# Folding the mean of a layer norm into the normalized activations instead of a rank-1 matmul, in a fused attention and FFN kernel

## What is computed

```python
m = mean(x); v = var(x); xn = (x - m) / sqrt(v + 1e-5)   # per token
q, k, v = xn @ Wq, xn @ Wk, xn @ Wv
att = softmax(causal(q @ k.T / 32)); a = LN(att @ v + v) * gamma + beta
x = x + LN(a @ Wfc + bfc)                                 # then the FFN part
```

## Time and profile before

| | us |
|---|---|
| median of the timed runs | 2835.54 |
| fastest of them | 2835.4 |
| the profiled execution's own time | 2833.55 |
| its span, slowest core (core 2) | 2831.9 |
| spans of the eight cores | 2817.3 to 2831.9 |

### The profile page before, as it was taken

The page is one execution under the profiler, slowest core; times in us unless marked ns, Lnnn a source line. Parts: engine busy times, 40 slices in busy tenths (PEclk is TensorE's granted clock), DMA queues, the critical chain, the costliest instruction groups (busy, mean ns, idle before and its releaser), DMA issues.

```text
span 2831.9 us, 36770 instructions; the slowest of 8 cores (2817.3 to 2831.9 us)
## 1 busy us (share of the span) xinstructions
PE 2305.4 (81%) x13009; PEld 1177.5 (42%) x13253; DVE 1057.7 (37%) x2187; ACT 498.2 (18%) x1026; POOL 61.6 (2%) x102
## 2 busy tenths in 40 slices
PE   2899999999999676567787897888888888889873
PEld 0233333333333243334344454554555555555541
DVE  0454554554554333434334323333222322232333
ACT  1010110110110012112122222222222222222210
POOL 0000000000000000000000000000000000000000
PEclk7899999999999788788798898999999999999985
DMA  9752552552541420203224244253526362654600
GB/s 177 151 138 106 150 138 104 148 133 106 148 134 60 145 93 31 89 30 105 75 90 164 75 149 149 89 195 118 209 95 221 115 223 102 211 179 151 206 31 15
DMA packets 75171, 357.58 MB, mean 126 GB/s; under 512 B 8832, under 2 KB 25728, under 8 KB 43248
## 3 DMA queue, kind: packets, MB, share of 16 engines
q1 hardware_dynamic: 50048, 276.84, 28.1%
q0 software_dynamic: 24944, 78.38, 12.1%
HBM read 324.51 MB, written 58.72 MB: 135 GB/s over the span
## 4 chain that ended last, share of the span: by engine, by line
PE 67%; DVE 19%; issue 5%; ACT 3%; DVEq 2%; another core or an unknown queue 2%; ACTq 1%; DMA 0%; POOL 0%; POOLq 0%
PE psBig L255 36%; PE psS L255 28%; DVE s_xhat L478 5%; DVEq L149 2%; DVE s_xovT L740 2%; DVE s_sm L711 2%; DVE s_sm L714 2%; PE psT L735 2%; PE psX L255 1%; DVE s_xov L727 1%; ACT s_sm L720 1%; DVE s_tscr L727 1%; DVE s_x1buf L972 1%; DVE s_x1buf L797 1%
## 5 line engine op out<-in xcount | busy, mean ns | idle before, releaser
L255 PE MATMUL psS<-s_qtile,s_ktile 128*128 128x256 bf16 x4352 | 599.9, 284 | 152.0 <-ACT s_ptb L1025 90.9
L255 PE MATMUL psBig<-s_vtile,s_ptb 128*128 128x512 bf16 x2026 | 551.6, 393 | 39.9 <-DVE s_ptb L1030 19.4
L255 PEld LDWEIGHTS psS<-s_qtile,s_ktile 128*128 128x128 bf16 x4352 | 403.6, 101 | 237.4 <-issue 178.8
L1025 ACT ACTIVATE s_ptb<-psS,s_cst 128x256 bf16<-128x256 f32 x544 | 257.6, 473 | 674.8 <-PE psS L255 661.9
L255 PE MATMUL psBig<-s_xhat,s_wk 128*128 128x512 bf16 x1000 | 276.9, 407 | 30.2 <-DVE s_xhat L478 27.9
L255 PEld LDWEIGHTS psBig<-s_vtile,s_ptb 128*128 128x128 bf16 x2176 | 216.0, 101 | 191.1 <-issue 56.8
L255 PE MATMUL psBig<-s_wv,s_xhat 128*128 128x512 bf16 x1000 | 240.7, 380 | 1.5 <-issue 0.6
L727 DVE TENSOR_SCALAR s_tscr<-s_astg,s_sm 128x1024 f32<-128x1024 f32 x64 | 52.0, 812 | 412.6 <-ACT s_sm L724 411.3
L508 DVE CAST s_kstg<-psBig 128x512 bf16<-128x512 f32 x192 | 132.7, 691 | 195.4 <-PE psBig L255 189.9
L255 PEld LDWEIGHTS psBig<-s_xhat,s_wk 128*128 128x128 bf16 x1024 | 93.4, 101 | 187.8 <-issue 111.5
L735 PE MATMUL psT<-s_identb,s_xov 128*128 128x128 bf16 x512 | 47.9, 249 | 146.2 <-DVE s_xov L727 146.2
(11 more groups left out here) (140 smaller groups left out, 1528.1 us busy)
## 6 DMA issues: line engine op xcount, KB each, us to landing
s_ktile<-kscr SPq DMA_DIRECT2D x88, 1024.0 KB, 5.5
s_vtile<-vscr SPq DMA_DIRECT2D x88, 1024.0 KB, 5.3
s_xs<-xkvC SPq DMA_DIRECT2D x16, 2048.0 KB, 13.4
s_xsbf<-xkvC POOLq DMA_DIRECT2D x16, 1024.0 KB, 15.0
s_xs<-xqC SPq DMA_DIRECT2D x8, 2048.0 KB, 14.7
kscr<-s_kstg SPq DMA_DIRECT2D x16, 1024.0 KB, 3.8
vscr<-s_vstg SPq DMA_DIRECT2D x16, 1024.0 KB, 3.9
s_x0g<-xq POOLq DMA_DIRECT2D x16, 1024.0 KB, 7.6
```

Source lines behind the costliest of these rows:

```text
L255: return lambda t: t.matmul(out=o, lhsT=l, rhs=r, start=start, stop=stop)
L1025: P.op("act", lambda e, psSm=psSm, m=m: e.activation(out=pt_ap(m), in_=psSm[:, 0:256], func=AF.Exp, scale=SCALE, bias=cst[:, 1:2]), reads= ...
```

## The change

The mean is taken off before the projections: after the multiplication by r, VectorE subtracts m·r from each chunk. For that `p0_xhat` spreads a second row, `r_mr`, over the partitions with another fp32 matmul of one row, into bank psS0, the bank of the sums of squares. The product goes to a new fp32 tile `xtmp` (one buffer for all chunks), and the difference to `xhat`. All that the old way needed is gone: the ninth matmul of each projection group, `plan_cw` with its three calls, and the bf16 row `r_mrb`. `hold_m` is fp32 now.

```diff
-            def plan_cw(wten, crow, wkey, ckey):
...
             def p0_rows(sl):
...
-                P.op("dve", lambda e: e.tensor_copy(out=rmrb,
-                                                    in_=r_mr[0:1, 0:512]),
-                     reads=["r_mr"], writes=[f"r_mrb{buf}"])
...
                 P.op("pe", MM(psS[1][:, 0:512], onesf[:], rrr, True, True),
                      reads=["onesf", "r_r"], writes=["psS1"])
+                P.op("pe", MM(psS[0][:, 0:512], onesf[:], r_mr[0:1, 0:512],
+                              True, True),
+                     reads=["onesf", "r_mr"], writes=["psS0"])
                 for i in range(NCH):
                     P.op("dve", lambda e, i=i: e.tensor_mul(
-                        out=xhat[:, buf * NCH * 512 + i * 512:
-                                 buf * NCH * 512 + (i + 1) * 512],
+                        out=xtmp[:],
                         in0=xs32[:, xo + i * 512: xo + (i + 1) * 512],
                         in1=psS[1][:, 0:512]),
                         reads=[f"xs{buf}", "psS1"],
+                        writes=["xtmp"])
+                    P.op("dve", lambda e, i=i: e.tensor_sub(
+                        out=xhat[:, buf * NCH * 512 + i * 512:
+                                 buf * NCH * 512 + (i + 1) * 512],
+                        in0=xtmp[:],
+                        in1=psS[0][:, 0:512]),
+                        reads=["xtmp", "psS0"],
                         writes=[f"xhat{buf}_{i}"])
...
-                            xh(i), i == 0, False),
+                            xh(i), i == 0, i == NCH - 1),
                             reads=[wkey, f"xhat{buf}_{i}"], writes=[bank])
-                    P.op("pe", MM(psBig[:, (o % 4) * 512:(o % 4 + 1) * 512],
-                                  crow[0:1, o * 128:(o + 1) * 128], rmrb,
-                                  False, True),
-                         reads=[ckey, f"r_mrb{buf}"], writes=[bank])
...
-                        P.op("pe", MM(psBig[:, bs:bs + 512],
-                                      rmrb[0:1, s4 * 128: s4 * 128 + 128],
-                                      cwv[0:1, h * 512:(h + 1) * 512],
-                                      False, True),
-                             reads=[f"r_mrb{buf}", "cwv"], writes=[bank])
...
                 p0_rows(slabs[0])
-                plan_cw(wk, cwk, "wk", "cwk")
                 p0_xhat(slabs[0])
-                plan_cw(wv, cwv, "wv", "cwv")
                 for t in range(nsl):
...
-                    if t == 0:
-                        plan_cw(wq, cwq, "wq", "cwq")
```

More of the change, by code:

```diff
@@ L343, in _plan @@
             wv = sb0("wv", [128, NCH * D], BF16)
-            cwq = sb0("cwq", [1, D], BF16)
-            cwk = sb0("cwk", [1, D], BF16)
-            cwv = sb0("cwv", [1, D], BF16)
             xs32 = sb0("xs32", [128, 2 * NCH * 512], F32)
@@ L358, in _plan @@
             r_mr = sb0("r_mr", [1, 512], F32)
-            r_mrb = sb0("r_mrb", [1, 1024], BF16)
             hold_r = sb0("hold_r", [1, 512], F32)
-            hold_m = sb0("hold_m", [1, 512], BF16)
-            def plan_cw(wten, crow, wkey, ckey):
[L364 to L374, removed]
+            hold_m = sb0("hold_m", [1, 512], F32)
+            xtmp = sb0("xtmp", [128, 512], F32)
             def p0_dma_xs(sl):
@@ L422, in p0_rows @@
                 if is_q:
-                    rmrb_ = r_mrb[0:1, buf * 512:(buf + 1) * 512]
                     P.op("dve", lambda e: e.tensor_copy(
@@ L426, in p0_rows @@
                         reads=["hold_r0", "hold_r1"], writes=["r_r"])
-                    P.op("dve", lambda e, rmrb_=rmrb_: e.tensor_copy(
-                        out=rmrb_, in_=hold_m[0:1, 0:512]),
-                        reads=["hold_m0", "hold_m1"], writes=[f"r_mrb{buf}"])
+                    P.op("dve", lambda e: e.tensor_copy(
+                        out=r_mr[0:1, 0:512], in_=hold_m[0:1, 0:512]),
+                        reads=["hold_m0", "hold_m1"], writes=["r_mr"])
                     return
@@ L433, in p0_rows @@
                 rrr = r_r[0:1, 0:512]
-                rmrb = r_mrb[0:1, buf * 512:(buf + 1) * 512]
                 P.op("dve", lambda e: e.tensor_scalar_mul(
@@ L490, in p0_proj @@
                                     buf * NCH * 512 + (i + 1) * 512]
-                rmrb = r_mrb[0:1, buf * 512:(buf + 1) * 512]
                 wten = wq if is_q else wk
                 wkey = "wq" if is_q else "wk"
-                crow = cwq if is_q else cwk
-                ckey = "cwq" if is_q else "cwk"
                 for o in range(NCH):
@@ L538, in p0_proj @@
                                 wv[:, i * D + h * 512: i * D + (h + 1) * 512],
-                                i == 0, False),
+                                i == 0, i == NCH - 1),
                                 reads=[f"xhat{buf}_{i}", "wv"],
                                 writes=[bank])
-                        P.op("pe", MM(psBig[:, bs:bs + 512],
-                                      rmrb[0:1, s4 * 128: s4 * 128 + 128],
-                                      cwv[0:1, h * 512:(h + 1) * 512],
-                                      False, True),
-                             reads=[f"r_mrb{buf}", "cwv"], writes=[bank])
                         P.op("dve", lambda e, s4=s4, h=h, bs=bs:
```

## The result

| | before | after |
|---|---|---|
| median, us | 2836.12 (10 runs) | 2914.38 (9 runs) |
| ratio | | 1.027, 95% interval 1.0249 to 1.029 |
| profiled execution, its own time, us | 2833.55 | 2911.72 |
| end of phase 0, mean of the eight cores, us | 939.2 | 1013.6 |

The change makes the kernel 2.7% slower; 2915 us were forecast. In some executions of any of these kernels the cores of one die are granted a lower clock and the time is longer, so the ratios leave those executions out, and where few are left the fastest run is given too. The end of phase 0 is taken from here on as the start of the first matmul behind its last slab, the first that reads `s_bt`, in each core's trace; on core 2 before the change that is 941.4 us, ahead of the fence that ends at 957. It moves by 74.4 us, and the rest of the program takes nearly what it took (1882 to 1892 us before, 1887 to 1895 us after).

The account below looks back on a forecast made before the run. Phase 0 was taken to run at TensorE's pace, except where VectorE makes the next slab's activations. −122.7 − 4.7 − 10.5 + 165.2 + 52.2 = +79.5 us on 2833.6 gives 2913.1, forecast 2915 us; range 2895 to 2940.

Parts of the forecast that it names:

- The ninth matmul at 0.41 us: In phase 0's projection groups: each one removed saves 0.413 us, 297 counted, 122.7 us less.
- The rival of one step: Removing a ninth matmul gives back only 0.217 us, 58 us fewer saved: 2973 us; chance 0.05.
- The pitch of the differences: VectorE's 16 operations at each slab border start 0.78 us apart; the last difference ends 13.7 us after the first spreading matmul.
- double rate: At slab borders the difference takes 0.27 us less, eight times at 23 borders, 50 us: 2865 us; chance 0.05.
- slower pairs: Chained product and difference at slab borders run at a pitch of 0.87 us, 31 us more: 2946 us; chance 0.07.
- The bank: At 14 borders with statistics the sums of squares wait on psS0 until 13.9 us; the second group starts 9.3 us later.
- The low clock: After TensorE's pause at 14 borders with statistics, 5 us at half rate lose 2.5 us each.
- The rival of a clock that holds: 10 us without a matmul does not lower the clock, 14 × 2.5 = 35 us go: 2880 us; chance 0.10.
- The start: Statistics of slab 1 no longer stand behind the column sums of wk and wv: 10.5 us earlier, range 8 to 11.
- VectorE's rows: Behind borders with statistics, copies start at 22.2 us, TensorE needs the bank at 25.1: 2.9 us of cover, no cost.
- A kv slab behind statistics: Its border costs 11.8 us, 9.3 from the later second group and 2.5 from the clock; 14 such borders, 165.2 us.
- a kv slab without statistics: Its border's second group starts at 14.3 us instead of 8.5: 5.8 us each, nine borders, 52.2 us.

Follow-up runs that it names:

- the filler: The changed kernel plus 40 matmuls of 512 columns that nobody reads, ahead of the sums of squares behind borders with statistics: 2891.89 us, ratio 1.019.

## Why the prediction was right

The forecast was 2915 us and the median is 2914.38. Its steps, one by one:

- **The ninth matmul at 0.41 us.** Right. Groups now start 1.72 to 1.73 us apart, 0.42 less than before; removing them alone gives about 0.41 us each once the wait for the copies is added, and doubling them shows that half of it is the change of shape. The rival of one step is out.
- **The pitch of the differences.** Right: 0.77 us on average (0.76 and 0.78 in turn) against 0.78. The rivals with a double rate and with slower pairs are out: 0.688 us for each.
- **The bank.** Right in place and size: 13.8 us against 13.9, at 14 borders; and the run with a bank of its own gave 44 us back, as worked out.
- **The low clock.** The mechanism is right and shown by the filler; the term was too large, 2.5 us against 1.9. The clock came back earlier behind the pause (0.60 over 5.2 us, so about 4 us at half rate) than in the row that I took it from (5 us). This makes 14 × 0.6 = 8 us. The rival of a clock that holds is out.
- **The start.** The term of 10.5 us is where the working failed. Slab 0 started 4.1 us earlier in the mean of the cores (81 to 85 us against 84 to 90), on single cores from 1.8 us later to 7.1 earlier. I had asked what no longer holds the first slab and not what is released earlier: its `xhat` is done at 46 us instead of 79, the load of slab 2 follows at once, and it shares the DMA engines with the weights. Held back, it disturbs the next load instead.
- **VectorE's rows.** Right that they cost nothing after the change: the copies start 22.15 us behind the spreading matmul, forecast at 22.2. The 2.9 us of cover leave out the 0.69 us of the first copy itself, which changes nothing. The same copies would have cost 16 us if the ninth matmuls had gone alone, so that the change hides a wait that its saving alone would meet.

By slabs the sum reads so. A kv slab behind statistics was forecast at 11.8 − 15 × 0.413 = +5.6 us and measured at +4.9; a q slab at 11.8 − 7 × 0.413 = +8.9 against +8.3; a kv slab without statistics at 5.8 − 15 × 0.413 = −0.4 against −0.5. Together 8 × (−0.5) + 7 × (4.9 + 8.3) = +88 us, where the forecast had +98. The start and the first slab gave less than forecast, by about 5 us. The two misses point opposite ways, so the total, +74.4 us at the end of phase 0 against +79.5, is nearer than its parts. The medians moved by 78.3 us, 4 more than phase 0. Phase 1 is 2.2 us longer in the mean of the profiled cores, where the forecast had it untouched, and no run here explains that. So the mechanism carried the forecast to within 5 us; that the median came within 1 us of it is luck.

## What to carry to other kernels

Before moving work off the busiest engine, look at what that engine does at the moment the new work runs. Here TensorE's 0.41 us each, spread over a slab, were traded for VectorE's 6.2 us in one piece at a border where TensorE can only wait, and a shared PSUM bank made even the work that could run beside it wait. If a correction is linear, put it into the weights once: that took both costs away and gave 0.96 of the time. And a copy or a load that comes free earlier can hold up another: the row ahead of the saved wait, and the one behind it, are part of the sum.

## What the runs showed of the hardware that I had not expected

- A matmul of one row between matmuls of 128 rows costs 0.41 us, of which 0.216 is the matmul and the rest the two changes: 0.31 us ahead of it and 0.32 behind it.
- Matmuls whose result nobody reads can pay. Forty in a pause of 10 us kept the granted clock at 1.00 and took 22 us off 2914.
- A load of 1 MB issued behind 6 MB of weights landed 48.9 us after its issue, and 50.2 us when the 4 MB queued behind it were held back.
